# Attention on one core: two passes share the adding of probabilities between GpSimd and VectorE, and a key's two copies go into two steps

## What is computed

```python
xn = _ln(x, norm_s_w, norm_s_b)
spatial_out = _spatial_experts(xn, idx_s, ...)        # softmax(q k^T) v, then a projection
xt = _ln(x, norm_t_w, norm_t_b)
temporal_out = _temporal_experts(xt, idx_t, ...)      # the same with a causal mask, plus xt
fused = _cross_mha(spatial_out, temporal_out, ...)    # queries of one, keys and values of the other
x = x + fused
h2 = _ln(x, norm_mlp_w, norm_mlp_b)
x = x + (gelu(h2 @ mlp_w1.T + mlp_b1) @ mlp_w2.T + mlp_b2)
```

## Time and profile before

| | us |
|---|---|
| median of 3 runs (lowest, highest) | 1836.44 (1834.28, 1839.62) |
| the profiled execution | 1838.64 |
| its span | 1836.6 |
| TensorE busy in it | 1652.5 (90%) |
| VectorE busy | 1066.6 (58%) |
| GpSimd busy | 875.5 (48%) |
| ScalarE busy | 711.8 (39%) |

### The profile page before, as it was taken

How to read it: one execution, slowest core, us unless ns; L and a number is a source line. 1 busy time by engine, 2 the same in 40 slices (tenths; PEclk the granted TensorE clock), 3 DMA queues, 4 the chain that set the end, 5 groups by cost and what they waited for, 6 DMA issues and landing times. The chain is left out here.

```text
span 1836.6 us, 32041 instructions
## 1 busy us (share of the span) xinstructions
PE 1652.5 (90%) x10735; PEld 1378.3 (75%) x10735; DVE 1066.6 (58%) x2221; ACT 711.8 (39%) x1346; POOL 875.5 (48%) x815
## 2 busy tenths in 40 slices
PE   2899988876899999999999997899999996899998
PEld 1788757755777888778878876788788874797896
DVE  7778768885556445654564562665555555683332
ACT  1223211114666445556555552464546553120010
POOL 3213001102587657684644466156566689383440
PEclk9999999988999999999999998899999998999999
DMA  3101000011031100030000000000000002121111
GB/s 116 35 7 47 12 1 29 18 49 50 12 125 41 35 19 7 1 130 12 18 13 7 7 1 24 17 19 7 7 13 13 1 1 85 40 74 35 46 35 56
DMA packets 24788, 58.06 MB, mean 32 GB/s; under 512 B 2537, under 2 KB 4805, under 8 KB 24013
## 3 DMA queue, kind: packets, MB, share of 16 engines
q1 hardware_dynamic: 24650, 56.18, 9.5%
HBM read 44.87 MB, written 11.30 MB: 31 GB/s over the span
## 5 line engine op out<-in xcount | busy, mean ns | idle before, releaser
L1801 DVE TENSOR_REDUCE max_part<-ps 125x2 f32<-125x500 f32 x520 | 328.1, 674 | 224.9 <-PE ps L2318 199.9
L1380 ACT ACTIVATE p_raw<-ps 125x500 f32<-125x500 f32 x520 | 296.9, 586 | 280.7 <-PE ps L2361 271.8
L1088 POOL TENSOR_TENSOR p_sum<-p_sum,p_raw 125x500 f32<-125x500 f32 x200 | 232.5, 1163 | 222.9 <-ACT p_raw L1380 215.7
L2376 PE MATMUL ps<-p_raw,v_rows 125*64 125x250 f32 x2080 | 248.5, 380 | 0.0
L1090 POOL TENSOR_TENSOR p_sum<-p_sum,p_raw 125x500 f32<-125x500 f32 x200 | 232.5, 1163 | 15.7
L2376 PEld LDWEIGHTS ps<-p_raw,v_rows 125*64 125x64 f32 x2080 | 143.4, 137 | 73.5 <-issue 4.5
L1641 DVE TENSOR_SCALAR onehot<-iota_h,win_key,key_t 125x320 f16 x453 | 176.9, 390 | 0.5 <-issue 0.4
L1817 DVE RECIPROCAL feat<-ps 128x250 f32<-128x250 f32 x60 | 103.0, 1717 | 113.8 <-PE ps L2386 113.6
L2260 PE MATMUL ps<-xa_hi,w_hi 128*128 128x418 f32 (+1 forms) x448 | 150.1, 335 | 14.5 <-POOL w_lo L954 9.1
L2357 PE MATMUL ps<-q_both_a,k_both_a 128*125 128x250 f32 x520 | 154.3, 317 | 9.4 <-ACT p_raw L1380 7.6
L2318 PE MATMUL ps<-k_both_a,q_both_a 128*125 128x250 f32 x520 | 143.8, 292 | 20.6 <-issue 9.1
(11 more groups left out here) (395 smaller groups left out, 3723.0 us busy)
## 6 DMA issues: line engine op xcount, KB each, us to landing
w_raw<-in_w_mlp SPq DMA_DIRECT2D x32, 256.0 KB, 2.7
w_raw<-in_w_gps SPq DMA_DIRECT2D x16, 256.0 KB, 2.6
w_raw<-in_w_tp SPq DMA_DIRECT2D x16, 256.0 KB, 2.6
w_raw<-in_w_sp SPq DMA_DIRECT2D x12, 256.0 KB, 2.7
w_raw<-in_w_cr SPq DMA_DIRECT2D x12, 256.0 KB, 2.6
d_xt<-xb_hi SPq DMA_DIRECT2D x1, 2508.0 KB, 9.4
d_xt<-xb_lo SPq DMA_DIRECT2D x1, 2508.0 KB, 15.0
xa_hi<-d_xt SPq DMA_DIRECT2D x1, 2508.0 KB, 9.3
```

Of the source, the lines that this page charges most:

```text
L1088: pool.tensor_tensor(total, total, halves[0], ALU.add).then_inc(s_add, 1)
L1380: act.activation(p_raw[:, g % PR, :], ps[0:TOK, g % 2, 0:4 * TOK], ACT.Exp, scale=SCALE).then_inc(s_exp, 1)
L1801: dve.tensor_reduce(part[:, y, :, j], ps[0:TOK, bank, 0:4 * TOK].rearrange("p (h k) -> p h k", h=2), AX.X, ALU.max)\
L2376: ins = pe.matmul(ps[r, bank, 0:2 * TOK], v_rows[:, n % 2, kt, h, :], p_raw[:, (g - 1 + h) % PR, cols], start=(b == 0 and x == 0), stop=last)
```

## The change

In passes 7 and 11 GpSimd adds the first head's probabilities alone (250 elements an instruction) and need not wait for the second head's exponent. VectorE adds the second head's (`add_second_head`), at the beginning of the step in which the pair is complete, with its own semaphore `s_add_b`, which the exponent eight steps on and the denominator wait for as well. In all passes `key_copy` copies one head's half: head 0's one step behind the key task as before, head 1's another step on (`third_out`).

```diff
+SHARED = (7, 11)
...
                 n, i, b, _ = STEP[g]
                 u, done = 5 * n + i, ADD_NO[n, i, b]
-                total = p_sum[:, u % 2, :, :]
-                halves = [p_raw[:, (g - 1) % PR:(g - 1) % PR + 2, 2 * TOK * x:2 * TOK * (x + 1)] for x in range(2)]
-                pool.wait_ge(s_exp, g + 1)
+                heads = 1 if n in SHARED else 2
+                total = p_sum[:, u % 2, 0:heads, :]
+                halves = [p_raw[:, (g - 1) % PR:(g - 1) % PR + heads, 2 * TOK * x:2 * TOK * (x + 1)] for x in range(2)]
+                pool.wait_ge(s_exp, g - 1 + heads)
...
-            def key_copy(n, p):
+            def key_copy(n, p, h):
...
-                for h, r in enumerate(HALF):
-                    ins = act.activation(k_both[h][HALF[1 - h], n % 2, cols], f32(k_both[h][r, n % 2, cols]), ACT.Copy)
-                ins.then_inc(s_k_both, 1)
+                act.activation(k_both[h][HALF[1 - h], n % 2, cols], f32(k_both[h][HALF[h], n % 2, cols]), ACT.Copy).then_inc(s_k_both, 1)
...
                     act.wait_ge(s_add, ADD_NO[n, i, b])
+                    if n in SHARED:
+                        act.wait_ge(s_add_b, SHARED_NO[n, i, b])
...
                 if what == "K":
-                    key_copy(*at)
+                    key_copy(*at, 0)
...
+            def third_out(task):
+
+                what, *at = task
+                if what == "K":
+                    key_copy(*at, 1)
...
+                    if g > first + 1:
+                        for task in SIDE[g - 2]:
+                            third_out(task)
...
+            def add_second_head(g):
+
+                n, i, b, _ = STEP[g]
+                u, done = 5 * n + i, SHARED_NO[n, i, b]
+                total = p_sum[:, u % 2, 1, :]
+                halves = [p_raw[:, g % PR, 2 * TOK * x:2 * TOK * (x + 1)] for x in range(2)]
+                dve.wait_ge(s_exp, g + 1)
+                if b == 0:
+                    dve.wait_ge(s_den, u - 1)
+                    dve.tensor_tensor(total, halves[0], halves[1], ALU.add).then_inc(s_add_b, 1)
+                else:
+                    dve.wait_ge(s_add_b, done - 2)
+                    dve.tensor_tensor(total, total, halves[0], ALU.add).then_inc(s_add_b, 1)
+                    dve.wait_ge(s_add_b, done - 1)
+                    dve.tensor_tensor(total, total, halves[1], ALU.add).then_inc(s_add_b, 1)
...
                 for g in range(first, end):
+                    if STEP[g][0] in SHARED and STEP[g][3] == 1:
+                        add_second_head(g)
...
-                pe.wait_ge(s_k_both, 3 * n + 3)
+                pe.wait_ge(s_k_both, 6 * n + 6)
...
                 pe.wait_ge(s_add, ADD_NO[n, i, blocks_in(n, i) - 1])
+                if n in SHARED:
+                    pe.wait_ge(s_add_b, SHARED_NO[n, i, blocks_in(n, i) - 1])
```

More of the change, by code:

```diff
@@ L182 @@
 ADDED = [(n, i, b) for n in range(PASSES) for i in range(5) for b in range(blocks_in(n, i))]
+SHARED = (7, 11)
+SHARED_NO = {(n, i, b): 2 * x + 2 - (5 * y + i + 1) for y, n in enumerate(SHARED) for x, (m, i, b) in
+             [(x, at) for x, at in enumerate(at for at in ADDED if at[0] in SHARED) if at[0] == n]}
 ADD_NO = {(n, i, b): 2 * x + 2 - (5 * n + i + 1) for x, (n, i, b) in enumerate(ADDED)}
@@ L717, in build @@
         s_add = sem("s_add")
+        s_add_b = sem("s_add_b")
         s_den = sem("s_den")
@@ L1426, in _ @@
                 query_hi(n, 0)
-                key_copy(n, 0)
-                key_copy(n, 1)
-                key_copy(n, 2)
+                for p in range(3):
+                    for h in range(2):
+                        key_copy(n, p, h)
                 value_feat(n, 0)
```

## The result

The changed kernel took 1828.11 us (median of 6 runs, 1826.84 to 1830.22), the kernel before 1837.15 in the same job (6 runs, 1834.28 to 1839.62): a ratio of 0.995, 95% interval 0.994 to 0.996, so 9 us faster. The forecast was 1822; the time lies 6 us above it and inside its range of 1813 to 1833. The profiled execution of the changed kernel took 1828.18 us (span 1826.2), 10.5 less than the 1838.64 of the one before, so the traces can be read for the whole difference.

What follows compares the result with a forecast made beforehand. TensorE, busy 90% of the span, was taken to bound the kernel. Gains of 10.4 (eighth pass), 2.3 (last pass) and 3.0 us (copies) summed to 15.7, giving 1822 us, range 1813 to 1833.

Steps and rivals of the forecast that it cites:

- The eighth pass: GpSimd's halved adds let unit 39's denominator start 7.4 us sooner and the low clock go: 10.4 us gained.
- The copies: One key copy moved a step on brings the next exponent 0.57 us sooner at ten waits: 3.0 us gained.
- largest case: Longest of ten TensorE waits for an exponent behind key copies: 2.60 us at 489.78.
- The last pass: Unit 57's wait goes, less stalls and a longer chain through VectorE at the end: 2.3 us gained.
- the stalls: Last pass: reductions queued behind VectorE's adds cost 0.8 us for each of three units, 2.5 us.
- unit 57's wait and slow stretch: TensorE's 4.53 us wait for GpSimd before unit 57's denominator and 2.1 us slow work behind it go: 6.6 us.
- The first: VectorE full in the last pass, adds 0.9 to 1.0 us, pass 3 to 8 us slower: 1828 to 1834; 17 in 100.
- The second: VectorE's adds and GpSimd shut each other out; slower, 1860 at 1.655 us an add, 1847 at 1.35; 7 in 100.
- the third: GpSimd's add hardly shortens, unit 39 still late, last pass pays for VectorE's adds: within 5 us; 9 in 100.
- the fourth: More than forecast: adds at 0.45 us, no stalls, copies' full 5.0 us: 22 us or more, under 1815; 12 in 100.
- The signs named ahead: Trace readings expected after the change, such as unit 39's wait under 2 us and VectorE over 90% busy.
- signs that the forecast had named for being wrong: Adds over 1 us, TensorE waiting for VectorE over 8 us in both passes, or unit 39 for GpSimd over 4.

Runs made afterwards that it cites:

- experiment 5: Second profiles of the eighth-pass-sharing-alone and split-copies-alone kernels: 3.48 and 1.95 us gained over the kernel before between the denominators of units 39 and 40.
- experiment 4: Changed kernel, bias additions held, last-pass sharing only for units 57 to 59: 1817.64 us; last kernel also moves VectorE's normalizations behind the last adds: 1816.01 us.

## Why the prediction was off where it was

The sum was 10.4 + 2.3 + 3.0 = 15.7 us; the ledger has 8.7 - 2.5 + 4.7 = 10.9. One of three terms has the wrong sign. That the other two come to 13.4 as forecast is luck: one is 1.7 short and the other 1.7 over, and much of both is the clock.

**The eighth pass: right in mechanism and nearly in size.** Forecast 10.4 us; 10.0 when done alone, 8.7 in the changed kernel. The denominator was forecast at 1120.0 and stands at 1119.77, but 1.1 us of that came with the copies ahead of the pass: the sharing moved it by 6.6 us (6.7 when alone), not by 7.4. GpSimd's add came out at 0.73, not 0.62, and VectorE's at 0.74, for 0.7. TensorE still waits 2.19 us for GpSimd there (forecast under 2), and VectorE's adds delay it by 0.7 us between the denominators of units 36 and 37 where 2.0 was forecast. These two errors cancel in part. The clock was forecast at 1 behind it; it was 0.76 for 7 us, the 1.4 us of experiment 5. The forecast's side remark that the term would be 12.6 us with adds of 0.42 doesn't follow from its own working: GpSimd's end at 1119.4 leaves 7.9 us, and 10.9 with the clock.

**The copies: undersized.** Forecast 3.0, "between 0 and 5"; 4.7 in the changed kernel. The part that the forecast reasoned about came out nearly as said: the waits at the scores fell by 3.4 us. But its largest case was misread. The wait of 2.60 us at 489.78 is put down to an exponent in the table of waits, yet ScalarE's timeline of before has that exponent done at 488.91 and two rows of maxima behind it, up to 489.68, just before TensorE goes on:

```profile
488.34 0.57 ACT L1380 ACTIVATE p_raw<-ps 125x500 f32<-125x500 f32 x1
488.93 0.37 ACT L1352 ACTIVATE q_row_a<-ps 1x250 fp32r<-1x250 f32 x1
489.31 0.37 ACT L1352 ACTIVATE q_row_b<-ps 1x250 fp32r<-1x250 f32 x1
```

Both copies still stand ahead of these rows in the changed kernel, and the wait is 2.74. The one of 0.89 us at 1211.17 is of the same kind. What the forecast left out is the clock. At 1321.18 the wait fell by only 0.7 us, from 1.79 to 1.09, but the stretch gained 2.2. The 6 us behind the wait, before and then now:

```profile
1321.18:1327.18 6.00, 6.00 (x36) 4.55 (x37) 1.74 (x3) 1.60 (x3) 4.62 (x4) 0.72 0.00 0
1309.72:1315.72 6.00, 6.00 (x50) 5.08 (x51) 2.53 (x4) 2.44 (x5) 4.94 (x5) 1.00 0.00 0
```

So 1.5 us of the 4.7 are a slow stretch that the shorter wait no longer leaves behind.

**The last pass: the step that failed.** Forecast was a gain of 2.3 us; it lost 2.5. Half of this miss of 4.8 lies in the pass: from unit 54 to unit 58 the gain was 1.8 instead of 4.1. The adds cost what they were said to cost, and the forecast said too that room and adds fall apart, but its 2.5 us for the stalls were too little. Of the 6.6 us for unit 57's wait and slow stretch 1.8 are left, so the stalls cost 4.8: 0.4 and 0.3 us in the intervals behind units 54 and 55, and 4.0 in the one behind unit 56, where TensorE waits 1.82 us and then works at a granted 0.76 up to 1512, 12.49 us busy with what took 10.43 before. The forecast had counted no clock for the stalls. Sharing the last three units alone gains 5.2 - 1.8 = 3.4 us more in the same stretch.

The other half lies in the tail. The forecast put "4 x 0.7 = 2.8" for its adds, the mean price, and took 1 us back at `oc_lo`, so 1.8 more; from unit 58's denominator to the projection 18.4 us before became 22.8, 4.3 more. The adds account for it: the four took 1.48 + 1.36 + 1.47 + 1.36 = 5.7 us, 2.9 over the 2.8, while the eight normalizations came to 8.4 us in sum, about the forecast's 8.7, by two errors that cancel: the first four took 0.67 each, less than forecast, the last four, beside the bias additions, 1.42, more than the 1.24 of before. The low parts came out as forecast. The forecast had seen that GpSimd would have most of its bias additions behind it when the low parts come, and took the gain from that, but didn't ask where they would lie instead: beside these adds. The row of 1.655 beside GpSimd's bias additions was the price for exactly this place, and with it the four adds come to 6.6 us instead of 2.8, and the last pass to a loss of 1.5.

**The rivals.** The first came true in sign for the last pass, and in total (1828 to 1834), but not as told: adds at 0.9 to 1.0 all through the pass were wrong, the mean is 0.74. The second, engines that shut each other out, holds where GpSimd's instruction is a long one: for the eight instructions of the tail and for the ten adds of over 1 us in the passes, not for the other 56. Against the third stands unit 39, which is no longer late; against the fourth, adds that cost 0.74 and not 0.45. The signs named ahead: unit 57's wait gone, VectorE over 90% busy with a new wait for max_part (one, 1.82 us), both so. Unit 39's wait was to be under 2 us and is 2.19; the clock behind it was to be near 1 and is 0.76 for 7 us. The 15 us from unit 58's denominator to unit 59's reciprocal are 1544.55 - 1526.60 = 17.95. And one of the signs that the forecast had named for being wrong came true: TensorE waits for VectorE by more than 8 us in the two passes, 11.53 at unit 59's denominator alone.

## What to carry to other kernels

When work moves off an engine, write down what that engine will start next and when: GpSimd's bias additions came 20 us earlier and fell beside VectorE's chain that TensorE waited for, and in the last kernel of experiment 4 its weight splits fell beside the next such chain. Price an instruction that can collide by the place where it stands, not by its mean: the same add was 0.42, 0.7 or 1.4 us by what its neighbour was doing. Look up in the timeline what ended a wait before counting on it: a releaser in the table of waits can be another instruction of the same engine. Count a wait together with the clock it leaves behind. And share work only where the backlog is (here the eighth pass and three units of the last), not over a whole pass whose average has room.

## What the runs showed of the chip

A short VectorE instruction on SBUF came out about as long as GpSimd's beside it, even one that reads one tensor and two columns of scalars: the normalizations went from 0.48 to 1.42 us beside additions of 1.41. The same 2.19 us of idle time on TensorE is followed by a granted clock of 0.76 in one kernel and 1.00 in another, and each repeats in a second profile; a wait of 1.79 us was followed by 0.72 over 6 us, one of 1.09 at the same place by 1.00. And profiles of one kernel repeat closely: the distance of 1048 to 1052 us came out within 0.2 us of its first value in all three kernels that were profiled twice.
